# Four part loads of the attention weights, an earlier second context, and a new order at two hand-overs of a two-layer kernel

## The reference

```
# layer 0, per sequence
xa = ln(x); sx = shifted(xa) - xa
r, k, v, g, w = products of xa + sx*(maa + adapters(xa, sx))
s_new = k v^T + w * s                  # a scan over the 112 tokens, per head
y  = group_norm(r . (faaaa*k v^T + s)) * silu(g)
x  = x + y @ Wo
xc = ln(x); x = x + sigmoid(xr2 @ fWr) * (square(relu(xk2 @ fWk)) @ fWv)
# layer 1, latents = x of layer 0, ctx = 375 rows per sequence
h = concat(ctx, latents)               # 487 keys
q = latents @ q_w + q_b;  k, v = h @ kv_w + kv_b;  16 heads of 32
a = softmax(mask(q k^T / 32)) v
z = a @ out_w + out_b + latents
out = gelu(rmsnorm(z) @ mlp_w1 + b1) @ mlp_w2 + b2 + latents
```

## Time and profile before

| | us |
|---|---|
| median of three runs | 1060.24 (1056.35 to 1061.8) |
| the profiled execution | 1062.83 |
| its span, first to last instruction | 1061.1 |

### The profile page before, as it was taken

The page is one execution under the profiler, slowest core; times in us unless marked ns, Lnnn a source line. Parts: engine busy times, 40 slices in busy tenths (PEclk is TensorE's granted clock), DMA queues, the critical chain, the costliest instruction groups (busy, mean ns, idle before and its releaser), DMA issues.

```text
span 1061.1 us, 17589 instructions
## 1 busy us (share of the span) xinstructions
PE 927.3 (87%) x6888; PEld 712.9 (67%) x6888; DVE 602.8 (57%) x1298; ACT 424.4 (40%) x957; POOL 227.4 (21%) x231
## 2 busy tenths in 40 slices
PE   4775788888888888679699999999999978999998
PEld 4664566666666666346478778787787846888886
DVE  2567889888989898962213432332343245545543
ACT  4111223232323233343265656666565556333332
POOL 2427344444444445400000000000000002000100
PEclk8876998989898989898899999999999989999999
DMA  6466333323242324100700101101010023000101
GB/s 223 115 204 225 131 104 79 105 70 114 76 145 73 110 69 107 53 18 1 272 1 8 52 3 54 46 9 47 8 54 1 10 86 127 0 0 27 43 0 35
DMA packets 34618, 77.10 MB, mean 73 GB/s; under 512 B 12590, under 2 KB 18734, under 8 KB 33519
## 3 DMA queue, kind: packets, MB, share of 16 engines
q1 hardware_dynamic: 34542, 76.07, 22.9%
HBM read 68.72 MB, written 7.34 MB: 72 GB/s over the span
## 4 chain that ended last, share of the span: by engine, by line
PE 51%; issue 21%; POOL 14%; DMA 5%; DVE 5%; ACT 3%; SPq 1%; POOLq 0%; DVEq 0%; ACTq 0%
POOL scan L450 9%; PE bank L1452 8%; PE bank L1575 8%; PE bank L1563 7%; PE bank L1446 6%; PE bank L1526 4%; PE bank L1467 3%; PE bank L1221 3%; PE bank L1518 3%; POOL xj L441 3%; DMA scan<-v_scratch 2%; PE bank L1548 2%; PE bank L1227 2%; PE bank L1481 2%; DMA v_scratch<-vt 1%
## 5 line engine op out<-in xcount | busy, mean ns | idle before, releaser
L749 DVE CUSTOM_DVE_ANT_0 smb<-bank,mask 112x487 f32<-112x487 f32 x128 | 78.6, 660 | 119.4 <-issue 119.4
L560 DVE TENSOR_TENSOR_SCAN scan<-bank,scan 128x448 f32<-128x448 f32 x128 | 132.1, 1073 | 9.9 <-POOL scan L453 9.9
L1221 PE MATMUL bank<-xj,front 128*128 128x112 f32 x1024 | 127.3, 287 | 11.1 <-POOL xj L441 11.1
L1221 PEld LDWEIGHTS bank<-xj,front 128*128 128x128 f32 x1024 | 124.6, 203 | 14.2 <-POOL xj L441 9.2
L450 POOL TENSOR_TENSOR scan<-scan,ks 128x896 f32<-128x896 f32 x64 | 125.7, 1964 | 26.1 <-DMA scan<-v_scratch 26.1
L1094 ACT ACTIVATE smb<-smb,nmax 112x487 f32<-112x487 f32 x128 | 88.5, 694 | 84.3 <-DVE nmax L749 84.3
L427 POOL TENSOR_TENSOR small<-small,neghalf 112x1 f32<-112x1 f32 x24 | 14.3, 594 | 475.3 <-DVE small L773 311.8
L567 DVE TENSOR_TENSOR scan<-scan,bank 128x896 f32<-128x896 f32 x64 | 69.4, 1084 | 3.1 <-DVE scan L560 0.5
L1526 PE MATMUL bank<-ident,smb 112*122 112x112 f32 x512 | 59.4, 265 | 4.7 <-ACT smb L1094 3.9
L1446 PE MATMUL bank<-cx_hi,kw_hi 128*128 128x488 f32 x128 | 53.1, 415 | 9.8 <-DVE cx_lo L639 9.8
L441 POOL TENSOR_TENSOR xj<-tmp,xa 128x448 f32<-128x448 f32 x40 | 41.6, 1058 | 90.9 <-DVE tmp L529 90.9
(11 more groups left out here) (180 smaller groups left out, 1946.2 us busy)
## 6 DMA issues: line engine op xcount, KB each, us to landing
scan<-v_scratch SPq DMA_DIRECT2D x64, 448.0 KB
w<-in_w SPq DMA_DIRECT2D x2, 4096.0 KB, 12.8
cx<-in_ctxt SPq DMA_DIRECT2D x8, 750.0 KB, 5.4
raw_w<-in_wbig SPq DMA_DIRECT2D x1, 4096.0 KB, 21.7
tail<-in_wbig SPq DMA_DIRECT2D x1, 3072.0 KB
front<-in_wbig SPq DMA_DIRECT2D x2, 1024.0 KB, 10.2
x_f<-in_x SPq DMA_DIRECT2D x8, 224.0 KB, 3.7
v_scratch<-vt SPq DMA_DIRECT2D x32, 56.0 KB, 1.8
```

The source lines that it names most:

```text
L560: n = v.tensor_tensor_scan(flat, decay, flat, 0.0, ALU.mult, ALU.add)
L749: v.tensor_tensor_reduce(sm[r], bank[r][0:T, 0:NKEY], mask_b[b % 2][:, :], -1.0 / DH, 3e38, ALU.add, ALU.min, nmax[:, h:h + 1]).then_inc(s ...
L1221: i = t_.matmul(tiles(dst)[:, m, :], w[:, k, m * P:(m + 1) * P], x[:, k, :], start=k == 0, stop=k == NT - 1)
```

## The change

No arithmetic is changed. What moves:

- **Loads.** The four attention matrices were one load of 4 MB after period 0; now each is a load of 1 MB, after periods 1 to 4. The first context's load moves from the end of period 4 to that of period 5. The second context and the first mask were loaded after the `w1` load; now before it. The load of `w2` no longer waits for the last latents' load (`load_latents(7)`).
- **Last scan (period 7).** `kv(0, 0)` and `kv(0, 1)` run on PE inside it; DVE makes kw's low half and the context's low half in it, and vw's afterwards; ACT splits the first context one period earlier.
- **Period after it.** `kv(0, 2)` to `kv(0, 7)`, and `query(0)` ahead of `hidden_values`; the second context is split there and no longer after it.
- **Start of the MLP.** On ACT the first Gelu, on DVE the first split and on PE the first `output_products` now stand ahead of the output projection of sequence 7.

```diff
-            def attention_weights():
-                sp.dma_start(raw_w[:, :, :, :], a["wbig"][:, 8:12]).then_inc(s["raw_loaded"], 16)
+            def attention_weight(n):
+                sp.dma_start(raw_w[:, n], a["wbig"][:, 8 + n]).then_inc(s["raw_loaded"], 16)
+
+            def output_bias():
...
-            attention_weights()
             for i in range(1, B):
                 period(i)
-                if i == 4:
+                if i < 1 + NT:
+                    attention_weight(i - 1)
+                elif i == 1 + NT:
+                    output_bias()
                     wait(sp, "pad_ready", 1)
                     load_context(0)
+            load_context(1)
             period(B)
+            load_mask(0)
             wait(sp, "ffn_ready", B)
             sp.dma_start(w1[:, :, :, :], a["w1"]).then_inc(s["w1_loaded"], 16)
-            load_context(1)
-            load_mask(0)
             period(B + 1)
             load_mask(1)
-            for b in range(B):
+            for b in range(B - 1):
...
             sp.dma_start(w2[:, :, :], a["w2"]).then_inc(s["w2_loaded"], 16)
+            load_latents(B - 1)
```

```diff
@@ tensor, period
                     decay_in(d)
+                if i == B - 1:
+                    kv(0, 0)
                 if real(a_):
                     hidden_keys(a_)
...
                     hidden_gate(a_)
+                if i == B - 1:
+                    kv(0, 1)
@@ tensor, kv
-                    pe.wait_ge(s["wsplit"], 2)
+                if b == 0:
+                    pe.wait_ge(s["wsplit"], 1 + n // NT)
+                if n < 2 and b == 0:
+                    pe.wait_ge(s[("gate_ready", "w_exp")[n]], B)
@@ tensor, last_period
                 means(a_)
-                kv(0, 0)
+                kv(0, 2)
                 variances(a_)
                 latents_turned(before)
-                kv(0, 1)
-                kv(0, 2)
-                block_output(a_)
                 kv(0, 3)
                 kv(0, 4)
+                kv(0, 5)
+                block_output(a_)
+                kv(0, 6)
                 second_turned(a_)
-                kv(0, 5)
+                kv(0, 7)
                 hidden_keys(a_)
                 hidden_gate(a_)
-                kv(0, 6)
+                query(0)
                 hidden_values(a_)
-                kv(0, 7)
-                query(0)
@@ tensor, after attention
-            output_projection(B - 1)
             pe.wait_ge(s["ri_kept"], B)
             for n in range(2):
                 g = n * NF
                 output_products(n, g, 0, start=True)
+                hidden_product(n, g + 2, 0)
+                if n == 0:
+                    output_projection(B - 1)
+                output_products(n, g + 1, 1)
                 if n == 0:
                     mlp_input(B - 1)
-                hidden_product(n, g + 2, 0)
-                output_products(n, g + 1, 1)
                 hidden_product(n, g + 3, 1)
```

More of the change, by code:

```diff
@@ L681, in period @@
                     gated(a_)
+                if i == B:
+                    out_bias()
+                    weight_low(2)
                 if real(d):
@@ L706, in period @@
                     weight_low(3)
+                    context_low(1)
                 if real(b):
@@ L819, in attention @@
                 inverse_sums(b)
-            context_low(1)
             mask(0)
[L823 to L826, removed]
             def split_hidden(g, p):
@@ L850, in step @@
                     w2_low(g + 1, 1 - p, (g + 1) % NF)
+            for b in range(B):
+                attention(b)
             w2_low(0, 0, 0)
-            step(0, 0)
+            split_hidden(0, 0)
+            attention_output(B - 1)
+            attention_low(B - 1)
+            w1_low(2, 0, 2)
+            w2_low(1, 1, 1)
             rms_start(B - 1)
+            split_hidden(1, 1)
             rms_end(B - 1)
-            step(1, 1)
+            w1_low(3, 1, 3)
+            w2_low(2, 0, 2)
             h1_low(3, 4, 8)
@@ L1045, in period @@
                     decays(d, 0)
-            for i in range(-1, B):
-                period(i)
+                if i == B - 1:
+                    kv_keep(0, 1)
             def kv_keep(b, n):
@@ L1063, in query_columns @@
                 columns(queries[b % 2], tiles(7), None, "q_b", "qt_ready")
+            for i in range(-1, B):
+                period(i)
             def last_period():
@@ L1067, in last_period @@
                 squares(a_)
[L1068 removed]
+                kv_keep(0, 2)
                 deviation(a_)
+                latent_columns(before)
+                kv_keep(0, 3)
                 norm_weights(a_)
[L1071 to L1073 removed]
+                kv_keep(0, 4)
                 weight_high(2)
[L1075 to L1076 removed]
+                kv_keep(0, 5)
                 second_columns(a_)
+                kv_keep(0, 6)
                 weight_high(3)
[L1079 removed]
                 relu_squares(a_)
+                kv_keep(0, 7)
                 second_gate(a_)
[L1082 to L1083 removed]
+                context_high(1)
                 query_columns(0)
                 latent_columns(a_)
[L1086 removed]
             last_period()
@@ L1176, in attention, with hidden @@
                     kv_keep(b + 1, 7)
-                keep_inverse(b)
[L1179 to L1183, removed]
-            def step(g, p, first=False, last=False):
+                else:
+                    act.wait_ge(s["w2_loaded"], 16)
+                    w2_high(0, 0)
+                    act.wait_ge(s["b1_loaded"], 16)
+                    hidden(0, 0, first=True)
+                keep_inverse(b)
+            def hidden(g, p, first=False):
                 act.wait_ge(s["hp_ready"], g + 1)
@@ L1190, in step @@
                               bias=b1v[:, bass.ds(g % NF, 1)]).then_inc(s["hid_ready"], 1)
+            for b in range(B):
+                attention(b)
+            attention_high(B - 1)
+            w1_high(0, 2)
+            w2_high(1, 1)
+            def step(g, p, first=False, last=False):
+                hidden(g, p, first)
                 if not last:
@@ L1196, in step @@
                     w2_high(1 - p, (g + 1) % NF)
-            act.wait_ge(s["b1_loaded"], 16)
-            step(0, 0, first=True)
             step(1, 1, first=True)
@@ L1422, in period @@
                     sum_pair(b, 3)
-            pe.wait_ge(s["init_pool"], INIT)
-            for i in range(-1, B):
-                period(i)
             def in_parts(w, x):
@@ L1488, in last_period @@
                 means(a_)
-                kv(0, 0)
+                kv(0, 2)
                 variances(a_)
                 latents_turned(before)
-                kv(0, 1)
-                kv(0, 2)
-                block_output(a_)
                 kv(0, 3)
                 kv(0, 4)
+                kv(0, 5)
+                block_output(a_)
+                kv(0, 6)
                 second_turned(a_)
-                kv(0, 5)
+                kv(0, 7)
                 hidden_keys(a_)
                 hidden_gate(a_)
-                kv(0, 6)
+                query(0)
                 hidden_values(a_)
-                kv(0, 7)
-                query(0)
                 latents_turned(a_)
+            pe.wait_ge(s["init_pool"], INIT)
+            for i in range(-1, B):
+                period(i)
             last_period()
```

25 lines of the change are left out of this document (13 added, 12 removed).

## The result

| | before | after |
|---|---|---|
| median, us | 1060.41 (8 runs, 1056.35 to 1064.09) | 1054.47 (8 runs, 1051.98 to 1058.41) |
| the profiled execution, its span | 1062.83, 1061.1 | 1056.6, 1054.9 |
| mean granted clock | 0.942 | 0.945 |

The ratio is 0.9943, with a 95% interval of 0.992 to 0.9967: 5.9 us less, between 3.5 and 8.5. The forecast was 1056.4.

A forecast was written before the change was run, and what follows sets the result against it. PE bounds attention, busy 49.83 of 50 us, so time could change only at the two hand-overs: entry -12.5 and MLP start +8.65 sum to -3.85 us, a median of 1056.4 us, range 1049 to 1064.

The forecast's parts named there:

- Loads: Periods 1 to 4: splitting the 4 MB weight load into parts changes the time by 0.
- Last scan: Last scan of layer 0: added kv products, less a faster hidden_keys, cost +0.6 us, between 0.4 and 1.4.
- The period after it: Period after the last scan: PE's 6.48 us gap is filled and the product behind it falls to 3.60: -6.5 us.
- The last store: Entry of attention: the store lands behind the w1 load, mask cleared 13.5 us after that load's issue, before 16.5.
- Rivals 2, 3 and 4: Entry: store passes weight load, 1049.7, chance 0.10; PE's gap little filled, 1060.2, 0.14; load holds store longer, 1065.3, 0.10.
- First maximum to `kv(1, 1)`: Entry of attention, from DVE's first maximum to kv(1, 1): -0.2 us, with 1.4 for half clock included.
- MLP (a): MLP start: first Gelu and its split ahead of keep_inverse make PE begin at 889.1, not 888.54: +0.55 us.
- (b): MLP start: second output_products waits for its split, queued on DVE behind rms_start(7); PE idles 2.7 us.
- (c): MLP start: mlp_input(7) moved back, one hidden_product covers its chain; PE waits 3.5 us before the third output_products.
- MLP (d): MLP start: the clock falls to half behind both new gaps, 1.5 us each: +3.0 us.
- rival 1: MLP start: the clock does not fall in the new gaps, start costs 5.65, total 1053.4 us; chance 0.24.
- POOL's additions, left out: MLP start: POOL's additions could slow the new second split by +1.0 us at most; left out of the sum.

The follow-up runs named there:

- e1: The kernel before with only the attention weights loaded in four parts after periods 1 to 4: 1061.12 us, ratio 0.9992.
- e2: The kernel before with only the MLP's first steps reordered and the second weight's load ahead of the last latents' read-back: 1069.17 us, ratio 1.0071.
- e8: The kernel before with only SP's order changed: second context, mask and last two stores ahead of the weight load: 1055.74 us, ratio 0.9945.
- e10: The kernel after with nine extra, unused matmuls in PE's gap ahead of the first output products: 1053.74 us, one execution.
- e11: The kernel after with the second hidden tile's split ahead of sequence 7's residual, and the third tile's activation and split earlier: 1048.47 us, ratio 0.9877.
- e6: The kernel after with DVE's split of the second hidden tile ahead of the residual of sequence 7: 1056.02 us, ratio 0.9947.
- e5: The kernel after with the last two stores of layer 0 issued ahead of the MLP's first weight load: 1044.74 us, ratio 0.9835.

## Why the prediction was right, by its own steps

- **Loads: 0.** Right within what can be told (e1: 0.9992). The 2.0 us that the traces show at that point are there in the start already, 2.60.
- **Last scan: +0.6.** By the two profiled executions 1.24. But e1, e2 and e8, which have the keys where before has them, take 32.4 to 32.7, and the mean of the four is 32.17 against 31.96 for the ten with the keys in the scan: -0.2. The 30.95 of the one execution I worked from was itself a short one. The term is too large by some 0.8, as far as four executions from 30.95 to 32.73 can say.
- **The period after it: -6.5.** From the last `y_cols` to the `w1` issue 46.78 before, 40.55 after: -6.2. The product behind the old gap takes the 3.60 us that were forecast (473.57).
- **The last store: cleared 13.5 us after the `w1` issue.** 13.75 (514.03 - 500.28), and from the issue to the first maximum 20.43 before, 14.15 after. Rivals 2, 3 and 4 are out for this order. The reason given was in part misread: of the 16.5 us before, the store spent 9.69 not yet issued, because SP was held by the mask's issue. The number held because both of its own parts did: 13.0 us for the weight (12.8) and 0.6 for the store behind it (0.7). The other end, "a store unhindered took 5.3 us", was mis-sized: it is 2.4.
- **First maximum to `kv(1, 1)`: -0.2.** Before 5.73, after 4.48 (518.91 - 514.43): -1.25. The term is mis-sized by a microsecond. The transposes began 1.55 us after the first maximum and kept up with the exponentials: 4.5 us to `kv(1, 1)`, forecast 4.1. It is the clock's 1.4 us that did not come: `kv(1, 1)` took 2.94 us for 2.82. Whether it comes is again open: in e10 and e11, with the same order, that product took 4.3, and their entry is 63.3 for some 62.1.
- **MLP (a) +0.55:** from `weighted(7, 3)` to the next product of PE 3.04 before, 3.61 after: +0.57. **(b) 2.7:** 2.48. **(c) 3.5:** 3.46. Both by the chain named: e6 removes the first, e11 the second.
- **MLP (d), clock, +3.0:** right for the profiled execution, where the three groups of twelve products after the gaps took 4.41, 4.03 and 4.43 us for 2.8. As a fixed price it was not: the falls come and go. The last gap, 3.46 us or more, was followed by one in all five executions that have it, that of 2.48 in three of four, so rival 1, no fall behind either, was seen in none of these. Old order: of seven executions, the four with an MLP of 175.6 or more take 8.2 us from the projection to the transposes, the other three 7.1. New order: three, two and one slow groups in after, e2 and e5, the one of e5 with 5.26 us for 2.8. By the means, 183.3 against 175.1, the whole start costs **+8.2**, predicted 8.65.
- **POOL's additions, left out:** rightly. The split (885.66, 0.63) began before the addition at 886.01; `rows_y`, 0.2 us behind it, took 1.51, and in e6 `hid_hi`, beside them too, 1.46 for 0.39. The Trainium skill (SBUF — State Buffer, SBUF: two separate sides) gives the port pair that VectorE and GpSimd share to whichever instruction starts first; these rows agree. Where the order of the MLP is mended, in e11, the lengthened splits beside them come to 1.7 us of wait.

**The sum.** The forecast's -3.85 lies inside the measured interval, -3.5 to -8.5, so its distance of 2.1 us to the median may be nothing. By the means of the stages the change is worth -0.2 in the last scan, -13.5 in the entry and +8.2 in the MLP, -5.5: the terms of the last scan and of the first maximum (0.8 and 1.1) and the MLP's 0.5 are what the forecast lacks, against some 0.5 too much in the two terms between. In the two profiled executions alone the two hand-overs come out at -12.4 and +8.9, forecast -12.5 and +8.65. That closeness is in part luck: the last scan there is 0.6 worse than forecast, and the way to `kv(1, 1)` a microsecond better.

## What to carry to other kernels

A small transfer that something waits for goes ahead of a large one that nothing waits for yet: here one line in SP's order is worth 10 us. Before a product is moved ahead of another, read what stands in front of its inputs on the engines that make them; a move on one engine alone can turn a hidden chain into three gaps. And compare two profiled executions by stages that both programs share unchanged before crediting a difference to an edit.

## What the runs showed of the hardware

- The same first part of the program takes 86.26 to 95.11 us to the first `y_cols`, in 14 executions, and the granted clock differs there: in 20 to 25 us of the span it was 0.50 before and 1.00 after. It is not the whole reason: the shortest start, e2's, has 0.50 there too.
- The same gap is followed by a fall of the clock in some executions and not in others: that of 2.07 us in four of seven, that of 2.63 in three of six. In e1 a second fall came in three periods in a row, behind an idle time of PE of 1.07 us that was 0.85 where no fall came, at 1.6 us each.
- A store of 224 KB has landed 2.4 us after its issue with a load of 4 MB issued 1.6 us behind it, and 12.2 with that load issued 1.5 us ahead.
- Behind a load of 4 MB and a context of 974 KB in two loads, the issue of a load of 164 KB held SP for 7.3 us, in before and in e2; ahead of them it took 0.42.
